# A graph network on one core: the first stage's steps reordered, and its two products joined

## The reference

```python
h = jnp.maximum(_layernorm(x, axis=-1), 0.0)
x = x + _L0_gnn_ref(h, src, dst, Ws, attn_l, attn_r, gat_bias, h_bias)   # 4 attention layers
h = jnp.maximum(_layernorm(x, axis=-1), 0.0)
x = x + _L1_gnn_ref(h, edge_attr_64, src, dst, ...)                      # gated convolution
# one attention layer (H = 4 heads of D = 64):
fs = (h @ W).reshape(N_NODES, H, D)
el = einsum('nhd,hd->nh', fs, al); er = einsum('nhd,hd->nh', fs, ar)
e = leaky_relu(el[src_e] + er[dst_e], 0.2)         # edges and one self loop a node
alpha = softmax of e over the edges of a destination
out = segment_sum(alpha * fs[src_e], dst_e) + b, summed over the heads
```

## Time and profile before

| | us |
|---|---|
| median of three runs | 3179.8 |
| the profiled execution's own time | 3188.4 |
| its span | 3186.6 |
| busy: PE, DVE, POOL, ACT | 2305.1, 2230.3, 1434.1, 1248.8 |
| first stage, from the first load to the next block's first load | 62.6 to 568.6 |

### The profile page before, as it was taken

The page is one execution under the profiler, slowest core; times in us unless marked ns, Lnnn a source line. Parts: engine busy times, 40 slices in busy tenths (PEclk is TensorE's granted clock), DMA queues, the critical chain, the costliest instruction groups (busy, mean ns, idle before and its releaser), DMA issues. The chain is left out here.

```text
span 3186.6 us, 38276 instructions
## 1 busy us (share of the span) xinstructions
PE 2305.1 (72%) x10796; PEld 1490.8 (47%) x10796; DVE 2230.3 (70%) x3891; ACT 1248.8 (39%) x2599; POOL 1434.1 (45%) x1389
## 2 busy tenths in 40 slices
PE   1998888399899399898569898749967781110575
PEld 1766665255575255566345565425533330000564
DVE  4766665677776567687377687468889976664698
ACT  0332332144332144343134333124445547662586
POOL 5777775000577300377500177700067754777000
PEclk9999999999855599777589877569989975555898
DMA  2333333011453111254101155202233321222464
GB/s 60 105 102 101 100 96 84 13 47 46 105 125 87 16 37 46 70 143 113 25 23 46 52 133 134 41 20 79 79 74 71 73 55 35 65 72 64 146 199 141
DMA packets 310382, 248.80 MB, mean 78 GB/s; under 512 B 149840, under 2 KB 258639, under 8 KB 310154
## 3 DMA queue, kind: packets, MB, share of 16 engines
q1 hardware_dynamic: 266270, 197.56, 20.6%
q0 software_dynamic: 43904, 48.80, 8.7%
HBM read 125.76 MB, written 118.06 MB: 77 GB/s over the span
## 5 line engine op out<-in xcount | busy, mean ns | idle before, releaser
L933 POOL DMA_INDIRECT edge<-table,row_of_source x588 | 596.9, 1015 | 909.4 <-POOLq L753 731.2
L871 PE MATMUL banks<-scaled_t,w_heads 128*64 128x512 f32 x784 | 380.1, 607 | 0.0
L815 DVE TENSOR_TENSOR_SCAN wide<-keep,wide,banks 64x512 f32<-64x512 uint8 x196 | 249.5, 1273 | 185.9 <-issue 161.3
L1229 POOL DMA_INDIRECT edge<-table,row_of_x x196 | 226.3, 1155 | 305.9 <-POOLq L131 244.6
L849 ACT ACTIVATE ring<-wide 128x512 f32<-128x512 f32 x196 | 123.6, 630 | 425.4 <-DVE wide L815 425.4
L1073 ACT ACTIVATE wide<-h_new 64x512 f32<-64x512 f32 x147 | 92.6, 630 | 474.1 <-DVE h_new L1019 474.1
L981 PEld LDWEIGHTS banks<-w_edge_full,wide 128*128 128x128 f32 x1176 | 219.6, 278 | 122.7 <-issue 105.9
L1488 POOL DMA_INDIRECT node_rows<-rows_conv,scatter_row x196 | 218.9, 1117 | 118.8 <-ACT rows_conv L1526 68.2
L981 PE MATMUL banks<-w_edge_full,wide 128*128 128x72 f32 x1176 | 227.7, 360 | 54.9 <-DVE self_logit L1029 54.0
L878 PEld LDWEIGHTS banks<-w_row,ring 128*128 128x128 f32 x1568 | 190.4, 191 | 161.1 <-issue 149.3
L974 PE MATMUL banks<-wide,w_row 128*64 128x512 f32 x294 | 241.6, 920 | 19.4 <-DVEq L1006 10.1
(11 more groups left out here) (300 smaller groups left out, 4571.9 us busy)
## 6 DMA issues: line engine op xcount, KB each, us to landing
node_rows<-x_out SPq DMA_DIRECT2D x97, 256.0 KB, 2.6
wide<-node_rows SPq DMA_DIRECT2D x48, 512.0 KB, 3.6
table<-chain_rows SPq DMA_DIRECT2D x147, 136.0 KB, 2.2
table<-rows SPq DMA_DIRECT2D x147, 136.0 KB, 2.3
nodes<-in_x_dram SPq DMA_DIRECT2D x97, 128.0 KB, 2.5
table<-x_out SPq DMA_DIRECT2D x97, 128.0 KB, 2.4
out_dram<-n_soft SPq DMA_DIRECT2D x48, 256.0 KB, 2.1
sources<-src_pad SPq DMA_DIRECT2D x49, 196.0 KB
```

The lines of the kernel that those rows point to most:

```text
L815: v.tensor_tensor_scan(out=wide[0:D, bass.ds(g * GE + 1, GE)], data0=keep[:, s], data1=bank[2 + s][0:D], initial=wide[0:D, bass.ds(g * GE, ...
L871: last = t_.matmul(bank[2 + s][0:D], w_heads[:, l, pair], scaled_t[:, s, pair], start=pair == 0, stop=pair == 1)
L933: pool.indirect_dma_start(out=edge[:, at_tile], out_offset=None, in_=tables[l], in_offset=bass.IndirectOffsetOnAxis(ap=row_of_source[:, at ...
L1229: pool.indirect_dma_start(out=edge[:, tile, 0:D], out_offset=None, in_=tables[l], in_offset=bass.IndirectOffsetOnAxis(ap=row_of_x1[:, tile ...
```

## The change

The product with `w_chain` (64 rows, 204 columns) and the one with `w_edge0` (128 rows, 8 columns) become one with `w_first` (128 rows, 212 columns), which holds both, zero in rows 64 to 127 of the first 204 columns. The steps are put in another order with other lags: all steps of a group after its gathers stand in one turn (lag 1), except ACT's copy of the products and SP's save of them (lag 2), and source load, `reach` and `search` stand a turn ahead (lag 0). For that the search writes to banks 2 and 3 for even groups and 6 and 7 for odd ones. POOL's list is the same.

```diff
@@ -32,6 +32,8 @@
 L = 4
 ROW = D + H
 EDGE_W = D + 2 * H
+CHAIN_W = (L - 1) * ROW
+FIRST_W = CHAIN_W + 2 * H
 HALF = 98
 TILES = 2 * HALF
 TPG = 4
@@ -150,8 +152,9 @@
         w_row = mem(top, "w_row", [P, L, ROW])
         w_edge = mem(top, "w_edge", [D, L, EDGE_W])
         w_edge_full = mem(top, "w_edge_full", [P, L, EDGE_W])
-        w_edge0 = mem(top, "w_edge0", [P, 2 * H])
-        w_chain = mem(top, "w_chain", [D, L - 1, ROW])
+        w_first = mem(top, "w_first", [P, FIRST_W])
+        w_chain = w_first[0:D, 0:CHAIN_W].rearrange("p (l w) -> p l w", w=ROW)
+        w_edge0 = w_first[:, CHAIN_W:FIRST_W]
         w_node = mem(top, "w_node", [D + 1, D])
         const_h = mem(top, "const_h", [D, L + 1])
         const_row = mem(top, "const_row", [P, D])
@@ -339,7 +342,7 @@
                     link(v.tensor_copy(w_heads[r:r + D, :, h // 2, :], w_raw[r:r + D, :, h, :]))
                 v.wait_ge(ident_ready, 1)
                 link(v.memset(w_row[:], 0.0))
-                link(v.memset(w_edge0[:], 0.0))
+                link(v.memset(w_first[:], 0.0))
                 eye = ident[0:D, 0:D].unsqueeze(1).broadcast_to([D, L, D])
                 v.tensor_copy(w_row[0:D, :, 0:D], eye).then_inc(dve_step, 1)
                 v.tensor_copy(w_row[0:D, 0:L - 1, D:ROW], a_sum[0:D, 0, 1:L]).then_inc(dve_step, 1)
@@ -435,6 +438,7 @@
             sp_paced = sem(st, "sp_paced")
             block = st.enter_context(nc.Block())
             COMPARES = 4
+            pair_of = lambda k: 6 if k % 2 else 2
 
             @block.gpsimd
             def _(pool):
@@ -465,7 +469,7 @@
                                      chain_rows[:, l]).then_inc(chain_saved, 16)
 
                 sp.sem_inc(chain_saved, 16)
-                pipelined(sp, ((1, save_x), (4, save), (0, load)), slots=SLOTS)
+                pipelined(sp, ((0, load), (1, save_x), (2, save)), slots=SLOTS)
                 for s in range(SLOTS):
                     sp.wait_ge(x_saved[s], 16 * uses[s])
                 sp.wait_ge(chain_saved, 16 * ((L - 1) * G + 1))
@@ -515,7 +519,7 @@
 
                     v.wait_ge(searched, at(k))
                     tiles = bass.ds(k * TPG, TPG)
-                    found = banks[:, 6:8, 0:2 * (P + 2)].rearrange("p b (t q) -> p b t q", q=P + 2)
+                    found = banks[:, pair_of(k):pair_of(k) + 2, 0:2 * (P + 2)].rearrange("p b (t q) -> p b t q", q=P + 2)
                     mine = src_f[:, tiles].rearrange("p (b t) -> p b t", b=2).unsqueeze(3).broadcast_to([P, 2, 2, P + 1])
                     v.tensor_scalar(tiles_before[:, tiles].rearrange("p (b t) -> p b t", b=2), found[:, :, :, 0], -1.0, None, ALU.add)
                     for n, op in enumerate((ALU.is_le, ALU.is_equal)):
@@ -527,7 +531,7 @@
                     v.wait_ge(compared, k * COMPARES + COMPARES)
                     v.sem_inc(looked_up, 1)
 
-                pipelined(v, ((3, normalize), (2, variance), (2, look_up), (1, center), (1, reach)), slots=SLOTS)
+                pipelined(v, ((1, center), (0, reach), (1, variance), (1, normalize), (1, look_up)), slots=SLOTS)
 
             @block.scalar
             def _(s_):
@@ -556,15 +560,15 @@
                     tiles = bass.ds(k * TPG, TPG)
                     s_.wait_ge(edges_in_psum, at(k))
                     s_.wait_ge(chain_saved, k * (16 * (L - 1)) + 16)
+                    made = banks[:, 4:6, 0:2 * FIRST_W].rearrange("p b (t w) -> p b t w", t=2)
                     for n in range(2):
                         last = s_.activation(chain_rows[:, :, 2 * n:2 * n + 2].rearrange("p l t w -> p t l w"),
-                                             bank[4 + n][:, 0:2 * (L - 1) * ROW].rearrange("p (t l w) -> p t l w", t=2, w=ROW), ACT.Copy)
+                                             made[:, n, :, 0:CHAIN_W].rearrange("p t (l w) -> p t l w", w=ROW), ACT.Copy)
                     last.then_inc(rows_ready, 1)
-                    both = bank[5][:, 2 * (L - 1) * ROW:2 * (L - 1) * ROW + TPG * 2 * H].rearrange("p (t e) -> p t e", e=2 * H)
-                    s_.activation(edge[:, tiles, D:ROW], both[:, :, 0:H], ACT.Copy)
-                    s_.activation(self_logit[:, tiles], both[:, :, H:], ACT.Copy).then_inc(logits_ready, 1)
-
-                pipelined(s_, ((2, scales), (3, take), (4, edge_out), (1, squares)), slots=SLOTS)
+                    s_.activation(edge[:, tiles, D:ROW].rearrange("p (b t) h -> p b t h", b=2), made[:, :, :, CHAIN_W:CHAIN_W + H], ACT.Copy)
+                    s_.activation(self_logit[:, tiles].rearrange("p (b t) h -> p b t h", b=2), made[:, :, :, CHAIN_W + H:], ACT.Copy).then_inc(logits_ready, 1)
+
+                pipelined(s_, ((1, squares), (1, scales), (2, edge_out), (1, take)), slots=SLOTS)
 
             @block.tensor
             def _(t_):
@@ -582,25 +586,22 @@
                     t_.wait_ge(norm_t_ready, at(k))
                     t_.wait_ge(logits_ready, at(k, back=1))
                     for t in range(TPG):
-                        mine = norm_t[:, t * P:(t + 1) * P]
-                        width = (L - 1) * ROW
-                        t_.matmul(bank[4 + t // 2][:, (t % 2) * width:(t % 2 + 1) * width], mine[0:D], w_chain[:].rearrange("p l w -> p (l w)"),
-                                  start=True, stop=True)
-                        last = t_.matmul(bank[5][:, 2 * width + t * 2 * H:2 * width + (t + 1) * 2 * H], mine, w_edge0[:], start=True, stop=True)
+                        last = t_.matmul(bank[4 + t // 2][:, (t % 2) * FIRST_W:(t % 2 + 1) * FIRST_W], norm_t[:, t * P:(t + 1) * P], w_first[:],
+                                         start=True, stop=True)
                     last.then_inc(edges_in_psum, 1)
 
                 def search(k, g, s, turn):
                     t_.wait_ge(reached_ready, at(k))
-                    t_.wait_ge(looked_up, at(k, back=1))
+                    t_.wait_ge(looked_up, at(k, back=2))
                     for t in range(TPG):
-                        to = bank[6 + t // 2][:, (t % 2) * (P + 2):(t % 2 + 1) * (P + 2)]
+                        to = bank[pair_of(k) + t // 2][:, (t % 2) * (P + 2):(t % 2 + 1) * (P + 2)]
                         for n in range(4):
                             half, part = n // 2, n % 2
                             up_to = (HALF + 1, HALF)[half]
                             last = t_.matmul(to, reached[0:up_to, half, t * P:(t + 1) * P], steps[0:up_to, half, part], start=n == 0, stop=n == 3)
                     last.then_inc(searched, 1)
 
-                pipelined(t_, ((3, transposes), (4, edges), (1, search)), slots=SLOTS)
+                pipelined(t_, ((1, transposes), (0, search), (1, edges)), slots=SLOTS)
 
         got_mem.close()
 
```

## The result

| | before | changed |
|---|---|---|
| median, 20 runs each, us | 3189.27 (3177.26 to 3200.84) | 3177.84 (3166.32 to 3185.18) |
| ratio | | 0.9962 (95%: 0.9949 to 0.9975) |
| profiled span, us | 3186.6 | 3176.4 |
| next block's first load starts | 568.58 | 552.39 |
| behind it, to the end of the span | 2618.0 | 2624.0 |

The change makes the kernel 0.38% faster, 12.1 us (8.0 to 16.3) by the ratio, where 15.5 were forecast. The forecast time of 3164.3 us is missed by 13.5 us, and 9.5 us of that is the base: the three runs shown had a median of 3179.8, twenty have 3189.3. The twenty runs of a kernel spread over 19 to 24 us.

The account below looks back on a forecast made before the run. The prediction took POOL's gathers as the bound, 45 periods of 10.39 us, plus the stage's start and tail. Tail -19.0, start +3.5 and pace 0 gave -15.5 us, from 3179.8 to 3164.3 us, range 3150 to 3174.

Parts of the forecast that it names:

- Tail: Stage end: from T, when DVE begins the last group, to the next block, 13.55 us replaces 32.6, 19.0 less.
- One product: PE's products: one joined product a tile takes 3.25 us a group where 6.0 are spent, bounds 1.95 and 4.1.
- Start: Stage start: SP's first save of x waits behind the second load, so POOL restarts 3.5 us later (2.1 to 3.9).
- Does a turn fit: Middle of the stage: DVE's 7.3 us and PE's 6.2 us a turn fit in POOL's period of 10.39.
- POOL's pace: Gathers slowed under DVE instructions: surplus of 0.44 us a group changes by -6 to +7 us over the stage, taken as 0.
- Rivals 1 and 2: Gathers collide with DVE instructions more (3187 us, chance 0.05) or less (3149 us, chance 0.15).
- Sum: Whole stage: -19.0 for the tail, +3.5 for the start and 0 for the pace make -15.5 us.
- rival 3: Most of the gain is lost near the stage's ends, 6 to 9 us left: 3172 us, chance 0.16.
- rival 4: The tail gets no shorter, since a turn waits for something due only with the next group: 3183 us, chance 0.04.
- carried differences over: Base: the difference worked out on the profiled execution, 3188.4 us, was applied to the three runs' median, 3179.8, giving 3164.3.

Follow-up runs that it names:

- e2: Changed kernel with the two products a tile of the kernel before; tail 16.38 us, ratio to the kernel before 0.9963.
- e1: Changed kernel with SP's save of x ahead of the source load; POOL restarts at 68.33 us, ratio to the kernel before 0.9963.
- e9: Changed kernel plus three unread two-operand DVE subtractions a group, on a slow chip; 15 gathers starting under them have a mean surplus of 0.161 us.
- e10: Changed kernel plus three unread one-operand DVE sums a group, on a slow chip; 18 gathers starting under them have a mean surplus of 0.005 us.
- e11: Changed kernel with the table of means, sums and scales moved to a PSUM bank, ordinary chip; ratio to the kernel before 0.9916.
- e3: Kernel before with its order, lags and banks, but the joined product; tail 21.9 us, ratio to the kernel before 0.9977.
- e12: Changed kernel with table in PSUM, save of x before the source load, and group 0's centering before reach; 3156.93 us, ratio to the kernel before 0.9913.
- e7: Changed kernel with the table of means, sums and scales in PSUM, on a chip with late transfers; ratio to the kernel before 1.0024.

## Why the prediction was right in its steps and wrong in its time

- *Tail.* Forecast T + 13.55 in place of T + 32.6; measured 13.52 in all three profiles of the changed kernel. Right.
- *One product.* Forecast 3.25 us a group; the last group's takes 3.19, and e2 puts the joined product at 2.86 us of tail. Over the stage the 49 rounds take 1.65 to 3.19 us with a median of 2.59, since TensorE's level goes up and down (last section); the forecast had the lower level throughout. The Trainium skill, "TensorE: Matmul & The Clock Gate", Part 3 (The mechanism), says that a weight load overlaps a running matmul only where their row groups differ. By that the round would be 5.1 us, an estimate with the prediction's 0.26 us a load; no round of this shape in these profiles takes over 3.2, so the runs are against it.
- *Start.* Forecast 3.5 us later; measured 3.6 against the setup's end, by the means of POOL's first idle time. The mechanism was right as far as it went; e1 showed a second hold behind it.
- *Does a turn fit.* Right: POOL has no second stall in any profile, the period stays.
- *POOL's pace.* Taken as no change within -6 to +7 us; measured periods are 10.36 to 10.39 us in four profiles of before and 10.39 to 10.44 in three of the changed kernel, 1.5 us in all by the means. The prediction had this term only as a bound, so that it came out near 0 is partly luck. The mechanism behind it, which was only argued, is now shown by e9, e10 and e11: a gather that starts under a DVE instruction with two operands in the shared memory waits for it. The Trainium skill, "GPSIMD Engine Reference", section 8 (Key points), names contention with DVE instructions in a 2-port perf mode or with two SBUF inputs (SBUF is the shared memory); the runs agree on the second, and no run here shows whether the comparisons of `reach` are a case of the first. Rivals 1 and 2, more and fewer collisions, didn't come.
- *Sum.* The stage was forecast 15.5 us shorter and is 14.4 shorter by the means; of what is missing the pace, put at 0, is the largest part (+1.5). The ratio's 12.1 us holds the forecast in its interval (8.0 to 16.3); the two later ratios (0.9968 and 0.9974) put it nearer to 10. By the last of them alone, 8 us, rival 3 (6 to 9 us left) would fit, but the stage's 14.4 and the tail of 13.52 are against it and against rival 4.
- *The step that failed* is the one that "carried differences over" to the median of three runs, 3179.8 us, with a range of 3150 to 3174 that came from the terms alone. The profiled execution, 3188.4 us, was in fact the typical one: twenty runs have a median of 3189.3. The three runs lay 9 us apart, and no width was set aside for where their median stands. That step made 9.5 of the 13.5 us; the other 4 are the 15.5 us against the 11.4 by which the two medians of twenty differ. With the profiled execution as base the forecast was 3172.9, 5 us from the result; that this one execution stood at the median was chance as well, since the twenty reach from 3177 to 3201.

## What to carry to other kernels

Where one engine sets the period from the first group to the last, look at what comes before its first instruction and after its last: reordering the others is worth mainly that, and a step that is put a turn ahead to shorten the tail is paid for at the head. Look also at that engine's own single instructions, since a surplus of 0.05 us in each of 360, some 19 us in all, was as large as the tail's gain, and moving 64 numbers a partition removed more than half of it. When the gain is small, take the width of the base into the range: a difference may be known to 5 us while the median of three runs is not.

## What the runs showed of the hardware that was not expected

TensorE's level. In the kernel before the granted clock reads 1.00 through the whole stage, but its search takes 1.91 us where the changed kernel's takes 1.94 in a stretch at 0.50, the level of 1.2 GHz (522.0 to 524.8 us), and 1.11 in one at 1.00, the level of 2.4 GHz. So that column is not to be trusted in the stage of before. The changed kernel, whose PE is far less busy, does reach the upper level at times: a search and a round of products in such a stretch, a round at the lower level, and the clock around them.

```profile
111.04 1.11 PE L601 MATMUL banks<-steps,reached 99*128 99x130 bf16 x16
111.99 1.65 PE L589 MATMUL banks<-w_first,norm_t 128*128 128x212 f32 x8
...
524.89 3.14 PE L589 MATMUL banks<-w_first,norm_t 128*128 128x212 f32 x8
```

```profile
111.00:113.60 2.60, 2.60 (x26) 2.30 (x24) 2.49 (x6) 1.19 (x2) 1.99 (x3) 1.00 0.59 184
...
524.00:528.00 4.00, 4.00 (x19) 3.35 (x16) 1.28 (x3) 0.59 (x1) 3.09 (x4) 0.50 0.48 132
```

The same eight records take 3.14 us in the stretch at 0.50 and 1.65 in the one at 1.00. No 204-column record of before or of e2 is shorter than 0.54 us, while a joined record in the changed kernel can be 0.34 long and e3 has rounds of 1.67 us: it goes with the joined product and not with the order. On the path it was worth something in two tails: 1.4 us in e3's second round, and 0.5 in e12's, where the four transposes take 0.66 us in place of 1.11.

Chips differ more than the change does. On one the kernel before took 3540 and 3557 us (two runs) and on another 3599 (median of 23), where it took 3186 to 3192 on the others. On the latter of the two POOL waited up to 14.7 us for one save to land (e7), and a version that is 0.84% faster elsewhere was not faster at all. Why these chips are slower no run shows.
